# Image scores and probabilities in three transfers each, and a new order on all five engines with column sums and attended sums in runs on TensorE

## The reference

```python
# layer 0
out = merge(attend(q, k, v)) @ Wo.T + bo + residual
# layer 1
probs_t = softmax(q @ k_t.T * scale);  text_out = probs_t @ v_t
qsem = l2norm(einsum('bhst,bte->bhse', probs_t, text_ehs))
sem = einsum('bhse,bne->bhsn', qsem, l2norm(ip_ehs))
probs_ip = softmax(q @ k_ip.T * scale + 0.5 * sem) * spatial_mask
out = (text_out + probs_ip @ v_ip) @ W_out + b_out + residual
```

## Time and profile before

| | us |
|---|---|
| median of 3 runs (2472.25 to 2475.6) | 2473.29 |
| profiled execution, its own time | 2473.34 |
| its span, first to last instruction | 2471.8 |
| PE busy in the span | 2273.8 |
| DVE busy | 1699.8 |
| ACT busy | 1726.8 |
| POOL busy | 1593.7 |

### The profile page before, as it was taken

How to read it: one execution, slowest core, us unless ns; L and a number is a source line. 1 busy time by engine, 2 the same in 40 slices (tenths; PEclk the granted TensorE clock), 3 DMA queues, 4 the chain that set the end, 5 groups by cost and what they waited for, 6 DMA issues and landing times.

```text
span 2471.8 us, 90321 instructions
## 1 busy us (share of the span) xinstructions
PE 2273.8 (92%) x35896; PEld 1458.5 (59%) x35896; DVE 1699.8 (69%) x2860; ACT 1726.8 (70%) x2602; POOL 1593.7 (64%) x1056
## 2 busy tenths in 40 slices
PE   7899967999999999999999999999999999999984
PEld 5677744555555555556555555655556555556552
DVE  5534333777777777777777777777777777777763
ACT  3323325877777777778777778877787787787862
POOL 3212124777777777777777777777777777777762
PEclk9999978999999999999999999999999999999997
DMA  9677642444434444444444444444444444444431
GB/s 289 197 225 229 198 115 64 112 114 115 111 109 117 115 114 117 115 118 116 112 117 116 114 115 119 117 111 116 114 118 116 113 118 118 115 118 117 112 90 56
DMA packets 337787, 310.89 MB, mean 126 GB/s; under 512 B 180208, under 2 KB 280816, under 8 KB 337392
## 3 DMA queue, kind: packets, MB, share of 16 engines
q1 hardware_dynamic: 337392, 305.36, 44.0%
HBM read 164.66 MB, written 105.98 MB: 109 GB/s over the span
## 4 chain that ended last, share of the span: by engine, by line
PE 34%; DVE 18%; DMA 12%; ACT 8%; issue 6%; SPq 6%; POOL 1%; ACTq 0%; DVEq 0%; POOLq 0%
PE psum L933 8%; PE psum L1032 8%; DMA den<-ust 8%; PE psum L1016 6%; PE psum L995 5%; ACT ef L1121 5%; DVE mneg L1180 3%; DVE e L1202 2%; PE psum L936 2%; DVE sq L1221 2%; DVE ust L1269 2%; DVE outt L1280 2%; DMA pt<-p_dram 2%; PE psum L999 1%; PE psum L958 1%
## 5 line engine op out<-in xcount | busy, mean ns | idle before, releaser
L1348 POOL TENSOR_TENSOR e<-ef,eh 73x1024 f32<-73x1024 f32 x320 | 681.4, 2130 | 298.9 <-ACT eh L1136 261.9
L1121 ACT ACTIVATE ef<-psum 73x1024 f32<-73x1024 f32 (+1 forms) x640 | 628.5, 1012 | 104.8 <-PE psum L999 100.9
L1202 DVE TENSOR_TENSOR e<-psum,e 73x1024 f32<-73x1024 f32 x320 | 386.6, 1208 | 158.5 <-PE psum L1032 158.2
L1180 DVE TENSOR_REDUCE mneg<-psum 128x8 f16<-128x616 f32 (+3 forms) x512 | 448.2, 930 | 31.0 <-PE psum L958 30.2
L1032 PE MATMUL psum<-eh,gram 128*73 128x512 f16 x1280 | 337.6, 387 | 36.6 <-ACT ef L1121 12.7
L1016 PE MATMUL psum<-ef,values 128*32 128x256 f32 x5120 | 363.5, 389 | 8.0 <-DVE pip L1262 5.9
L995 PE MATMUL psum<-q_high,keys 32*73 32x256 f16 (+2 forms) x6144 | 325.5, 259 | 33.9 <-DVE mneg L1180 25.4
L1136 ACT ACTIVATE eh<-ef 73x1024 f16<-73x1024 f32 x320 | 337.0, 1053 | 16.4 <-ACT ef L1121 0.8
L995 PEld LDWEIGHTS psum<-q_high,keys 32*73 32x73 f16 (+1 forms) x6144 | 187.7, 111 | 143.6 <-issue 68.1
L1129 ACT ACTIVATE ust<-psum 128x512 f32<-128x512 f32 x384 | 228.2, 594 | 63.2 <-PE psum L1016 59.2
L1315 POOL TENSOR_TENSOR al<-ust,ah 128x768 f16<-128x768 f32 x128 | 210.7, 1646 | 86.6 <-ACT ah L1159 86.5
(11 more groups left out here) (180 smaller groups left out, 4659.7 us busy)
## 6 DMA issues: line engine op xcount, KB each, us to landing
rb<-r_dram SPq DMA_DIRECT2D x128, 384.0 KB, 3.8
keys<-k_dram SPq DMA_DIRECT2D x128, 231.0 KB, 3.7
values<-v_dram SPq DMA_DIRECT2D x128, 192.5 KB
ust<-ust SPq DMA_DIRECT2D x512, 48.0 KB, 2.1
v_dram<-vst SPq DMA_DIRECT2D x64, 320.0 KB
out<-outt SPq DMA_DIRECT2D x64, 320.0 KB, 2.3
k_dram<-kst SPq DMA_DIRECT2D x32, 616.0 KB, 3.9
x<-in_x SPq DMA_DIRECT2D x32, 384.0 KB, 3.7
```

The source lines that it names most:

```text
L1121: act.activation(ef[l][0:m, unit_heads(n), :].rearrange("t h s -> t (h s)"), src, ACT.Exp, scale=SM).then_inc(s_exp[l], 1)
L1180: dve.tensor_reduce(dst, o, AX_X, ALU.max, negate=True).then_inc(s_max[l], 1)
L1202: dve.tensor_tensor(rest, banks(l, f"u{k}", 2)[0:m, :, :], rest, ALU.mult).then_inc(s_wr, 1)
L1348: pool.tensor_tensor(e2[0:m, k, :, :], ef[1][0:m, unit_heads(k), :], eh[0:m, unit_heads(k), :], ALU.subtract).then_inc(s_e2, 1)
```

## The change

The diff, with one line of each table:

```diff
 ORDER = {
     "pe": """
-        1n0/3 1p/4 1n1/3 1n2/3 0s0/0 1n3/3 1n4/3 0s1/0 1t1/2 1a0/2 1u0/2 1t2/2 1u1/2 1o/4 0m/0 0o/1 0t0/0""",
+        1a2/4 1i/3 1u3/4 1m/3 1u4/4 1t0/3 1n0/4 1n1/4 1n2/4 1n3/4 1n4/4 1p/5 0q/1 1t1/3 1u0/3 0s0/1 1t2/3
...
 USES = [
-    "0t2/1 0t4/1 1s0/2 1s3/2 1t0/2 1p/4 0s3/0 1t4/2 0t0/0",
+    "1u3/4 1p/5 1u0/3 1t4/3 1o/5 0t1/1 0t3/1 0t4/1 1s0/2 1s2/2",
...
             def store_ip_scores(l, b, n):
                 b.reached(sp, s_sip, 1, 1)
-                dst = s_dram[b.parity()].rearrange("m (c s) -> c m s", c=CW)
-                sp.dma_start(dst, sipst[:, b.parity(), :]).then_inc(s_ss, 16)
+                for c in range(CW):
+                    sp.dma_start(s_dram[b.parity()][:, c * S:(c + 1) * S], sipst[c * SLOT:(c + 1) * SLOT, b.parity(), :])\
+                      .then_inc(s_ss, 16)
 
             def load_ip_scores(l, b, n):
                 b.reached(sp, s_y, STEPS, SIP_READ - STEPS)
-                b.reached(sp, s_ss, 16, 16)
+                b.reached(sp, s_ss, 16 * CW, 16 * CW)
...
             def load_ip_probabilities(l, b, n):
                 b.reached(sp, s_ps, 16, 16)
-                src = p_dram.rearrange("m (c s) -> c m s", c=CW)
-                sp.dma_start(pt[:], src).then_inc(s_pt, 16)
+                for c in range(CW):
+                    sp.dma_start(pt[c * SLOT:(c + 1) * SLOT, :], p_dram[:, c * S:(c + 1) * S]).then_inc(s_pt, 16)
...
             def attend_ip(l, b, n):
                 wait_free(pe, l, b, "p")
                 b.reached(pe, s_vb, 1, 1)
-                b.reached(pe, s_pt, 16, 16)
+                b.reached(pe, s_pt, 16 * CW, 16 * CW)
```

More of the change, by code:

```diff
@@ L125 @@
     "pe": """
-        1u2/3 1a1/3 0t1/1 1q/2 0t2/1 0a0/1 1s0/2 0a1/1 1s1/2 0a2/1 1i/2 1a2/3 1u3/3 1m/2 1u4/3 1t0/2 0q/0
-        1n0/3 1p/4 1n1/3 1n2/3 0s0/0 1n3/3 1n4/3 0s1/0 1t1/2 1a0/2 1u0/2 1t2/2 1u1/2 1o/4 0m/0 0o/1 0t0/0""",
+        1a2/4 1i/3 1u3/4 1m/3 1u4/4 1t0/3 1n0/4 1n1/4 1n2/4 1n3/4 1n4/4 1p/5 0q/1 1t1/3 1u0/3 0s0/1 1t2/3
+        1u1/3 0s1/1 1o/5 0m/1 0o/2 0t0/1 1u2/3 1a0/3 0t1/1 1q/2 0t2/1 0a0/1 1s0/2 0a1/1 0a2/1 1s1/2 1a1/3""",
     "act": """
-        1a1/3 1f/4 0t2/1 0t3/1 1q/2 0t4/1 1h4/3 0a0/1 0a1/1 0a2/1 1i/2 1a2/3 1m/2 0r/0 1t0/2 1h0/2 0q/0
-        1t1/2 1h1/2 1n/3 1g/4 1t2/2 1t3/2 1a0/2 0g/1 1t4/2 1h2/2 0m/0 1r/2 1h3/2 0t0/0 0t1/0""",
+        1a1/4 1a2/4 1i/3 1m/3 0r/2 1t0/3 1h0/3 1t1/3 1n/4 1h1/3 1g/5 0q/1 1t2/3 1t3/3 1t4/3 0g/2 1h2/3 1h3/3
+        1h4/3 0m/1 1r/3 0t0/1 0t1/1 1a0/3 0t2/1 0t3/1 1f/4 1q/2 0t4/1 0a0/1 0a1/1 0a2/1""",
     "dve": """
-        1y11/4 0o/2 1y12/4 1y13/4 1y14/4 1w2/3 1y15/4 1y16/4 1y17/4 1y18/4 1y19/4 1ql/2 1s0/2 1s1/2 1s2/2
-        1s3/2 1w3/3 0d/1 1w4/3 1d/3 0ql/0 1p/4 0s0/0 0s1/0 0s2/0 0s3/0 1w0/2 1w1/2 1y0/3 1y1/3 1y2/3 1y3/3
-        1o/4 1y4/3 1y5/3 1y6/3 1y7/3 1y8/3 1y9/3 1y10/3""",
+        1s1/3 1s2/3 1s3/3 1w3/4 0d/2 1w4/4 1p/5 1d/4 0ql/1 1w0/3 0s0/1 0s1/1 0s2/1 0s3/1 1y0/4 1o/5 1w1/3
+        1y1/4 1y2/4 1y3/4 0o/2 1y4/4 1y5/4 1y6/4 1y7/4 1y8/4 1y9/4 1y10/4 1w2/3 1y11/4 1y12/4 1y13/4 1y14/4
+        1y15/4 1y16/4 1y17/4 1y18/4 1y19/4 1ql/2 1s0/2""",
     "pool": """
-        1xh/2 1xl/2 1b3/3 1b4/3 0xh/0 0xl/0 1vb/4 1kb/1 1at/4 1c/2 1b0/2 1b1/2 1al/4 0at/1 0al/1 1b2/2""",
+        0xh/1 0xl/1 1b0/3 1b1/3 1al/5 0at/2 1kb/2 0al/2 1c/3 1b2/3 1xh/2 1xl/2 1b3/3 1at/4 1vb/4 1b4/3""",
     "sp": """
-        1ss/3 1sl/3 1rl/4 1sh/4 0x/0 1vi/4 1ps/4 0ds/1 1v/2 1pl/4 1ds/3 0k/0 1g/2 0rw/1 0sh/1 0rl/1 1c/1
-        1ns/3 1rw/3 1nl/3 1k/1 1d/3 1st/4 0v/0""",
+        0ds/2 1pl/5 0k/1 1ds/4 1g/3 1v/3 0rw/2 0sh/2 0rl/2 1ns/4 1sl/4 1rw/4 0v/1 1nl/4 1d/4 1st/5 1ss/3
+        1k/2 1sh/4 1rl/4 1ps/4 1vi/3 1c/2 0x/0""",
 }
 USES = [
[8 rows of a table removed]
[8 rows of a table added]
 ]
```

## The result

The changed kernel took 2497.5 us in the median of five runs (2493.6 to 2502.4), the kernel before 2472.3 beside it. The ratio is 1.0106, with a 95% interval of 1.0092 to 1.012. It is slower, as forecast (2488), by 25 us in place of 15. The profiled execution of the changed kernel, its slowest of the five, spans 2500.8 us, 29.0 more than before's 2471.8.

What follows compares the result with a forecast made beforehand. Before, PE bounds the cycle up to `1u1` and DVE from there to `1u2`. From 2473.3 us, 61 x 0.38 = 23.2 up and 8.6 down gave 2488; 0.8 range 2450 to 2510, likeliest case 2478 to 2505.

Steps and rivals of the forecast that it cites:

- `1t2` waits for `w0`: On PE behind `1u0`: `1t2` reuses banks 4 and 5, so it idles about 0.9 to 1.2 us for DVE's `w0`.
- `0s1` for an exponential: On PE: `0s1` reuses banks 6 and 7, so it idles 0.3 us until ACT's exponential `1t4` ends.
- Rival (a): PE still closes the cycle, new holds costing no more than old: 2444 to 2458, 2452 in the middle; chance 0.22.
- the clean cycle, 32.0 forecast: Steady-state cycle without slips, `1u2` to `1u2`: 32.0 us against 31.62, 0.38 more, with bounds 31.4 and 32.3.
- the stretch to `1t1`: PE from `1u2` to the start of `1t1`: 19.8 us, before 20.22; up to 0.4 shorter if runs pipeline better.
- DVE's work from the maxima to `1u2`: DVE from the maxima of parts 2 and 3 to `0o`, without a gap, closes the cycle: 25.6 to 32.0 us.
- (c): Rival: stretch to `1t1` 0.3 us shorter, holds stay; clean cycle 31.7, time 2470 us; chance 0.15.
- "costing SP nothing": On SP: the split transfers add 1.8 us a cycle, landing in time SP has (196 us of waiting in 62 cycles).
- the 8.6 us gained: PE's slips from late transfers, 4.7 us at the queries (`xl`) and 3.9 at `p`, counted as gained.
- The orders: The new step orders with their bank holds lengthen 61 cycles by 0.38 us each: 23.2 us up.
- Rival (d): `0ds`, behind the 384 KB load of x, comes late for `w4`; 1 us late gives 43 more, 2531; chance 0.10.
- Its own wait: On PE: a wait at `n` (last column sum) for DVE's `w4`; its appearance would show the forecast wrong; no size given.

Runs made afterwards that it cites:

- e2: The changed kernel with the image scores and the image probabilities each in one transfer again, all orders kept; 2472.6 us, ratio 1.0003.
- e6: The changed kernel with only the scores' store split, the probabilities in one transfer; 2499.5 us, ratio 1.0100.
- e1: The changed kernel with only SP's list reordered (`0k` ahead of `1pl`; `1vi`, `1c`, `1v` behind `0rl`), both splits kept; 2475.2 us, ratio 1.0008.
- e4: The kernel of e1, with its reordered SP list, but both transfers single; 2472.9 us, ratio 1.0000.
- e5: The kernel before with only `1sl` moved in SP's list, from directly behind `1ss` to behind `1ns`; 2464.3 us, ratio 0.9966.
- e11: The kernel of e5 (kernel before, `1sl` moved) with both transfers split; 2479.0 us, ratio 1.0018.
- e3: The kernel before with both transfers split, its orders and banks untouched; 2475.1 us, ratio 1.0017.

## Why the prediction was right, and where it was not

**Right: slower, and the waits it named.** `1t2` waits for `w0` (0.84 in the clean cycle; forecast 0.9 to 1.2), and `0s1` for an exponential (0.18; forecast 0.3). The wait at `1t1` is gone, the column sums are one run of 2.37 (2.44), the wait at `p` is gone, and SP no longer waits for stored scores. PE is faster up to `1u0` and gives it back at the banks, as forecast. Rival (a) fell as it was said to: `1t2` did wait.

**Wrong: the clean cycle, 32.0 forecast, 31.67 measured.** The term that was mis-sized is the stretch to `1t1`: 1472.46 - 1453.02 = 19.44, not 19.8, within the bound that I gave it. It makes all of the difference, for from `1t1` to `1u2` the cycle takes 12.23 (1484.69 - 1472.46), and 12.2 was forecast. Inside that last stretch a second error changed who closes the cycle, and hardly its length. DVE's work from the maxima to `1u2` held `y0` at 0.85. In the changed kernel's clean cycle the DVE timeline reads:

```profile
1478.34 2.15 DVE L1181 TENSOR_REDUCE mneg<-psum 128x12 f16<-128x924 f32 x2 [1.08 <-PE psum L965]
1480.40 0.20 DVE L1222 TENSOR_SCALAR sq<-n 96x64 f32<-96x64 f32 x1
1480.78 0.82 DVE L1281 SCALAR_TENSOR_TENSOR outt<-psum,res 128x640 f32<-128x640 f32 x1 [0.18 <-PE psum L937]
1481.53 1.21 DVE L1203 TENSOR_TENSOR e<-psum,e 73x1024 f32<-73x1024 f32 x1
...
1483.67 0.96 DVE L1281 SCALAR_TENSOR_TENSOR x1a<-psum,res 128x768 f32<-128x768 f32 x1 [0.28 <-PE psum L934]
```

`y0` takes 0.20, and DVE waits 0.28 for PE ahead of `0o`. So DVE does not close the cycle without a gap; PE closes it, by way of `0o`. By the forecast's own sum PE's `0o` ends at 30.8, and here DVE's `0o` starts 0.14 behind it. That would be 30.94 in place of 31.0, so no more than 0.1 of the forecast hung on `y0`. Of the rivals (c), a clean cycle of 31.7, was the true one, and its 2470 is close to e2, the kernel without the splits (2472.6).

**Wrong: "costing SP nothing", and the 8.6 us gained.** This is the step that failed. The gain came (the waits for `xl` and the probabilities, 8.6 us before, are 1.3), but the transfers cost 25 us where I had nothing. I had asked when the split transfers themselves are used, and found them early. I had not asked what stands behind them on SP: `ss` ahead of `1rl`, through POOL's `at` and `vb` to `1vi`, and `pl` ahead of `0rw`. The 196 us of SP's waiting that the change removes were taken as slack for the 1.8 us a cycle, though they lie at another place of the list. The splits were dear by place more than by length: in SP's time they cost 0.6 each as a rule (1.37 and 1.38 against 0.79 and, in e2, 0.7), less than the 0.9 forecast. What the forecast did not know of is the single part that holds SP for up to 2.3 us.

Here a page had a word for the change. The Trainium skill, Perfetto Trace Analysis, section DMA Optimizations, says that splitting may let some of a transfer start sooner, and the whole task end sooner if the DMA engines are largely idle. The runs agree for the part's own reader (the wait at `p`, 15.9 us in e6, none in the changed kernel) and not for the task, in any of the pairs (e1 and e4, e2 and after, e5 and e11, before and e3). The DMA engines were not largely idle here: their share in a cycle before was 0.43.

**So the number was near by luck.** The orders were forecast at +23 us and were worth 0 (e2); the transfers at -8.6 and were worth +25. Two errors of opposite sign left 25 where 15 was forecast.

Rival (d) named the right resource, a transfer late through SP's row, but as the main loss another load (the denominators of `0d`); the one that cost most is the inverses of `0rl`. Its own wait appeared as well, which the prediction had named as a sign of being wrong. In the slipped cycle shown above:

```profile
1595.03 0.55 DVE L1196 RECIPROCAL rd<-den 96x64 f32<-96x64 f32 x1 [1.18 <-DMA den<-ust]
```

`w4` stands behind this `0d`, and PE waits for it at the column sums, 3.5 us in 6 cycles here and 8.6 in 11 in e6 (before: 0.9, once). But `0ds` was not late for the reason given, the load of x ahead of it: it stood behind `1vi`, which waited for `vb`. It is the same chain, with a second reader.

## What to carry to other kernels

A transfer that is cut into parts costs its issuing queue once for each part, and the price is paid by whoever waits for the entries behind it: walk the queue's list behind the split to the next thing that is awaited, through the engines that release the queue's own waits, before calling it hidden. Put the parts ahead of an entry on which the queue waits anyway. When the mean cycle is longer and the shortest one is not, look for a chain with no slack, not for a dearer instruction.

## What the hardware showed that was not expected

**A short DVE instruction that stretches until a POOL instruction ends.** `y0`, 96 x 64 elements, waits for the norms' load. Its durations (ns, shortest, median, longest), 400 to 2400 us, in the kernel before:

```profile
L1221 DVE TENSOR_SCALAR sq<-n x62: 180/847/1672, 443.4 to 2387.1; 96x64 f32<-96x64 f32 x62
```

In the changed kernel the median is 448, and in e1 181. The same instruction on the same data takes 180 ns or up to nine times as long. A late load would be the first guess. But in the changed kernel's clean cycle it began 4.3 us behind the load's issue (1476.14) and took 0.20, and before it began 3.9 behind it (2096.93) and took 0.85. What goes with the long records is POOL. The instruction that ran there in the cycle of the earlier trace rows:

```profile
2100.01 1.65 POOL L1315 TENSOR_TENSOR al<-ust,ah 128x768 f16<-128x768 f32 x1 [1.10 <-ACT ah L1159]
```

It ends at 2101.66, and `y0`, begun at 2100.85, ends at 2101.70. Of the 62 records before, 59 are longer than 190 ns, and every one of them ends 0.05 us behind the end of the POOL instruction that ran when it began. In the changed kernel it is 45 of 61, again every one. So a long `y0` is one that began while POOL was at work, and it lasts until POOL is done. No run moved POOL's work to test it, but the match leaves little room. DVE's `w1`, which reads a bank of PSUM as well, is not stretched: it ran beside the same `al` in its 1.22. Taken for work, it put 0.65 us of waiting into the prediction's sum.
